# A recommendation tower on one core: the last chunk in two halves of 128 batches

## The reference

```
e = stack([tbl_f[ids[:, f]] for f in range(26)], axis=1)
sd = einsum('bfd,bd->bf', e, dense);  ss = einsum('bfd,bgd->bfg', e, e)
z = concat([dense, sd, ss[:, iu, ju]], axis=1);  h = concat([z, dense], axis=1)
h = max(h @ W_top1 + b_top1, 0);  h = max(h @ W_top2 + b_top2, 0);  y = h @ W_top3
```

## Time and profile before

| what | value |
|---|---|
| median of three runs | 566.14 us |
| profiled execution | 558.6 us, its span 556.8 us |
| TensorE, matmuls (PE) | 401.6 us busy, 72% of the span |
| TensorE, weight loads (PEld) | 361.3 us busy, 65% |
| ScalarE (ACT) | 211.6 us busy, 38% |
| VectorE (DVE) | 186.7 us busy, 34% |
| GpSimd (POOL) | 258.0 us busy, 46%, nearly all gathers (264) |
| mean granted TensorE clock | 0.859 of full speed |

### The profile page before, as it was taken

The page is one execution under the profiler, slowest core; times in us unless marked ns, Lnnn a source line. Parts: engine busy times, 40 slices in busy tenths (PEclk is TensorE's granted clock), DMA queues, the critical chain, the costliest instruction groups (busy, mean ns, idle before and its releaser), DMA issues.

```text
span 556.8 us, 9727 instructions
## 1 busy us (share of the span) xinstructions
PE 401.6 (72%) x3976; PEld 361.3 (65%) x3976; DVE 186.7 (34%) x684; ACT 211.6 (38%) x312; POOL 258.0 (46%) x270
## 2 busy tenths in 40 slices
PE   2603957777449869787849895688749887597898
PEld 2602856677338858577737895487747876496776
DVE  3503934263201544034420462124520355132300
ACT  3402733344313343334333352335334344255422
POOL 6774866336752266614664256524665256300000
PEclk9955896888778898879888997789888898799699
DMA  7951133325210152102511053102521042102030
GB/s 184 249 136 52 44 82 102 109 55 150 60 38 25 36 143 69 46 13 64 149 47 39 21 132 88 40 25 47 146 69 38 21 107 86 29 3 66 25 87 2
DMA packets 44509, 40.70 MB, mean 73 GB/s; under 512 B 29943, under 2 KB 36335, under 8 KB 44464
## 3 DMA queue, kind: packets, MB, share of 16 engines
q1 hardware_dynamic: 36016, 22.75, 15.8%
q0 software_dynamic: 8448, 17.32, 12.0%
HBM read 34.29 MB, written 5.76 MB: 72 GB/s over the span
## 4 chain that ended last, share of the span: by engine, by line
PE 53%; another core or an unknown queue 15%; issue 14%; ACT 8%; DVE 6%; DMA 2%; SPq 1%; DVEq 0%; ACTq 0%
PE oh_ps L590 23%; PE dot_ps L609 14%; PE mlp_ps L634 7%; DVE onehot L518 5%; PE mlp_ps L645 4%; PE tr_ps L575 4%; ACT feat L418 3%; ACT feat L423 2%; PE mlp_ps L653 1%; ACT ids_bc L407 1%; DMA dots<-tbl_dram 1%; DVE table_lo L505 1%; DMA dots_scratch<-rows 1%; ACT h L438 1%
## 5 line engine op out<-in xcount | busy, mean ns | idle before, releaser
L382 POOL DMA_INDIRECT rows<-tbl_dram,idx_sb x264 | 257.5, 975 | 220.8 <-PE tr_ps L575 101.2
L518 DVE TENSOR_SCALAR onehot<-ids_bc 125x256 fp32r<-125x256 int16 x608 | 137.9, 298 | 159.6 <-issue 53.6
L590 PE MATMUL oh_ps<-onehot,table_hi 125*128 125x256 f32 x608 | 106.8, 324 | 63.6 <-issue 30.8
L590 PEld LDWEIGHTS oh_ps<-onehot,table_hi 125*128 125x128 f32 x608 | 90.8, 220 | 70.8 <-issue 37.5
L423 ACT ACTIVATE feat<-oh_ps 128x256 f32<-128x256 f32 x76 | 51.8, 690 | 157.9 <-remote 66.5
L590 PE MATMUL oh_ps<-onehot,table_lo 125*128 125x256 f32 x608 | 96.2, 305 | 2.3 <-issue 2.1
L609 PE MATMUL dot_ps<-feat 128*54 128x52 f32 x2048 | 77.1, 235 | 23.2 <-issue 21.4
L590 PEld LDWEIGHTS oh_ps<-onehot,table_lo 125*128 125x128 f32 x608 | 88.6, 214 | 3.5 <-issue 3.1
L609 PEld LDWEIGHTS dot_ps<-feat 128*54 128x54 f32 x2048 | 69.6, 150 | 31.8 <-issue 27.6
L418 ACT ACTIVATE feat<-tr_ps 128x512 f32<-128x512 f32 (+1 forms) x72 | 82.5, 1146 | 15.4 <-remote 9.3
L527 DVE COPY dots<-dot_ps 54x416 f32<-54x416 f32 x56 | 32.2, 593 | 161.4 <-remote 123.4
(11 more groups left out here) (26 smaller groups left out, 72.6 us busy)
## 6 DMA issues: line engine op xcount, KB each, us to landing
dots_scratch<-dots SPq DMA_DIRECT2D x28, 175.5 KB
rows<-tbl_dram,idx_sb POOLq DMA_INDIRECT x264
ids_bc<-ids_t_dram SPq DMA_DIRECT2D x12, 256.0 KB
feat<-tbl_dram SPq DMA_DIRECT2D x6, 480.0 KB
zt<-dots_scratch SPq DMA_DIRECT2D x14, 117.0 KB
dots<-tbl_dram SPq DMA_DIRECT2D x3, 480.0 KB
ids_bc<-ids_t_dram SPq DMA_DIRECT2D x4, 320.0 KB
dense_sb<-dense_f_dram SPq DMA_DIRECT2D x8, 128.0 KB
```

The source lines that it names most:

```text
L382: nc.gpsimd.indirect_dma_start(rows[:, g, t, :], None, tables[UNIT[par][u][k]], bass.IndirectOffsetOnAxis(ap=idx_sb[:, par, g * TILES + t: ...
L518: last = nc.vector.tensor_scalar(onehot[0:TP, lookup_place(u), c, :], ids_bc[0:TP, u, :], float(c), None, ALU.is_equal)
L590: last = nc.tensor.matmul(lookup_psum(u), part[0:TP, u, c * D:(c + 1) * D], onehot[0:TP, lookup_place(u), c, :], start=(part is table_hi a ...
```

## The change

The last chunk is cut into two halves of 128 batches. Its gathers are issued for all units' first halves (t = 0) and then for the second (t = 1); a second half waits for nothing else on GpSimd. New step letters stand for its parts: a0 to a8 and b0 to b8 transpose and copy the first and the second half of each unit; e0 to e7 are its dot products, of which e0 to e3 make the first half and e4 to e7 the second; p0 to p5 are chunk 6's MLP; q and t are the MLP of the first and of the second half, with products that move 128 batches. `SLOT_LAST` now holds all of it and the three lists behind it are gone. SyncE stores and loads each half by itself (`make_last_z`), with the same number of DMAs for each half as before for the whole chunk but the dense load, which is issued once, ahead. Chunk 7's dots are copied to `dots` instead of `rows`, after chunk 6's stores from there have landed. On the host, the dense features and the outputs of the last chunk are reordered to match.

```diff
-SLOT_LAST = "m0 m1 r0 m2 m3 r1 m4 d0 d1 m5 d2 d3 l5 r2 d4 d5 l6 d6 d7 l7 r3 l8 r4 f r5 r6 r7 r8"
-DOTS = "d0 d1 d2 d3 d4 d5 d6 d7"
-MLP = "m0 m1 m2 m3 m4 m5"
+SLOT_LAST = ("m0 m1 m2 m3 m4 d0 d1 m5 d2 d3 l5 a0 d4 d5 l6 a1 d6 d7 l7 a2 l8 f a3 a4 a5 a6 a7 a8 e0 e1 e2 e3 "
+             "p0 b0 p1 b1 b2 p2 b3 p3 b4 b5 p4 b6 b7 p5 b8 e4 e5 e6 e7 q0 q1 q2 q3 q4 q5 t0 t1 t2 t3 t4 t5")
...
+        def columns(half):
+            return slice(0, CH) if half is None else slice(half * P, (half + 1) * P)
...
         def dots_of(h, par):
-            if isinstance(h, int) and chunk(h, par) == NCH - 1:
-                return rows[:].rearrange("p f t d -> p (f t d)")[:, 0:PACK * NJ * QS]
             return dots[:]
...
+            def make_last_z(half):
+                h, par = NCH // 2 - 1, 1
+                z, done = z_of(h, par), GUNITS * (NCH - 1) + GUNITS // 2 * (half + 1)
+                if half == 0:
+                    sp.wait_ge(dots_out_act, GUNITS * (NCH - 1))
+                    sp.dma_start(z[:, ZC, :], dense_t[NCH - 1:NCH].rearrange("a p b -> (a p) b")
+                                 ).then_inc(last_z_loaded[half], DMA)
+                sp.wait_ge(dots_out_act, done)
+                sp.wait_ge(dots_out_dve, done)
+                products = dots_dram[par, 0:NI * NJ, columns(half)].rearrange("(i j) b -> i j b", j=NJ)
+                w = QS // 2
+                for q in range(Q):
+                    row = TILE * (q // PACK) + NI * (q % PACK)
+                    own = dots[row:row + NI].rearrange("p (k j g) -> p k j g", k=PACK, j=NJ)
+                    sp.dma_start(products[:, :, q * w:(q + 1) * w],
+                                 own[:, q % PACK, :, half * w:(half + 1) * w]).then_inc(dots_stored, DMA)
+                sp.wait_ge(dots_stored, Q * DMA * (NCH + half))
+                for c in range(ZC):
+                    i0, m = c * ZI, min(ZI, NF - 1 - c * ZI)
+                    runs = dots_dram[par, i0 * (NJ + 1) + 1:(i0 + m) * (NJ + 1) + 1, columns(half)]
+                    sp.dma_start(z[0:m * DIST, c, columns(half)],
+                                 runs.rearrange("(i d) b -> i d b", d=NJ + 1)[:, 0:DIST, :]
+                                 ).then_inc(last_z_loaded[half], DMA)
...
+            def last_gathers(h, par):
+                pool.wait_ge(idx_loaded[par], DMA * (h + 1))
+                for t in range(TILES):
+                    for u in range(UNITS):
+                        if t == 0:
+                            pool.wait_ge(transposed, (chunk(h, par) - 1) * UNITS + u + 1)
+                        for k in range(len(UNIT[par][u])):
...
+            def last_transposed_to_feat(u, t):
+                act.wait_ge(transposed, (NCH - 1 + t) * UNITS + u + 1)
+                fs = UNIT[1][u]
+                m, step = len(fs), fs[-1] - fs[0]
+                nc.scalar.activation(feat_view(1, fs[0] + 1, m, max(step, 1))[:, :, t * P:(t + 1) * P],
+                                     tr_ps[:, 0:m, t * P:(t + 1) * P], ACT.Copy).then_inc(transposed_out, 1)
...
+            def last_transposes(u, t):
+                par, loads = 1, [DMA * TILES * len(UNIT[p][u]) for p in range(2)]
+                if t == 0:
+                    pe.wait_ge(rows_loaded[u], sum(loads) * (NCH // 2 - 1) + loads[0] + loads[par] // TILES)
+                else:
+                    pe.wait_ge(late_rows_loaded[u], loads[par] // TILES)
+                pe.wait_ge(transposed_out, (NCH - 1 + t) * UNITS + u)
...
             def dot_products(h, par, v):
                 n = chunk(h, par)
+                if n == NCH - 1 and v == GUNITS // 2:
+                    pe.wait_ge(transposed_out, UNITS * (NCH + 1))
...
-            def layer1(h, par, x):
...
+            def layer1(h, par, half, x):
+                n, cols = turn(h, par, half), columns(half)
                 if x == 0:
-                    if n < NCH - 1:
+                    if half is None:
                         pe.wait_ge(z_loaded, DMA * Z_DMAS * (n + 1))
                     else:
-                        pe.wait_ge(last_z_loaded, DMA * Z_DMAS)
+                        pe.wait_ge(last_z_loaded[half], DMA * (Z_DMAS - half))
```

More of the change, by code:

```diff
@@ L162, in z_of, with turn, h2_half @@
             return zt[:]
-        def h2_half(h, par, x):
-            return z_of(h, par)[:, x, :]
+        def columns(half):
+            return slice(0, CH) if half is None else slice(half * P, (half + 1) * P)
+        def turn(h, par, half):
+            return chunk(h, par) + (half or 0)
+        def h2_half(h, par, x, half):
+            return z_of(h, par)[:, x, columns(half)]
         def lookup_place(u):
@@ L182, in dlrm_tower @@
         rows_loaded = [sem(f"rows_loaded{u}") for u in range(UNITS)]
+        late_rows_loaded = [sem(f"late_rows_loaded{u}") for u in range(UNITS)]
         dense_loaded = sem("dense_loaded")
@@ L204, in dlrm_tower @@
         z_loaded = sem("z_loaded")
-        last_z_loaded = sem("last_z_loaded")
+        last_z_loaded = [sem(f"last_z_loaded{x}") for x in range(2)]
         l1_done = sem("l1_done")
@@ L444, in relu2, with output @@
                                      bias=b2_sb[:, x:x + 1]).then_inc(h2_made, 1)
[L446 to L449, removed]
+            def output(h, par, half):
+                n, cols = chunk(h, par), columns(half)
+                t0, t1 = cols.start // P, cols.stop // P
+                act.wait_ge(l3_done, turn(h, par, half) + 1)
+                nc.scalar.activation(y_sb[:, n * TILES + t0:n * TILES + t1], mlp_ps[:, 0, t0:t1],
@@ L481, in run @@
                         mlp_step(*old, x)
+                    if kind in "ab":
+                        last_transposed_to_feat(x, "ab".index(kind))
+                    if kind == "p":
+                        mlp_step(*done, x)
+                    if kind == "e":
+                        dots_to_sbuf(*rows, x)
+                    if kind in "qt":
+                        mlp_step(*rows, x, "qt".index(kind))
             act.wait_ge(iotas_made, 1)
@@ L524, in dots_to_sbuf @@
                 dve.wait_ge(dots_done, n * GUNITS + v + 1)
-                if v == 0 and not (isinstance(n, int) and n in (0, NCH - 1)):
+                if v == 0 and n:
                     dve.wait_ge(dots_stored, Q * DMA * n)
@@ L576, in transposes @@
                 last.then_inc(transposed, 1)
+            def last_transposes(u, t):
[5 more added lines that the diff above has]
+                pe.wait_ge(transposed_out, (NCH - 1 + t) * UNITS + u)
+                for k in range(len(UNIT[par][u])):
+                    last = nc.tensor.transpose(tr_ps[:, k, t * P:(t + 1) * P], rows[:, 2 * u + k, t, :], ident[:])
+                last.then_inc(transposed, 1)
             def lookup(h, par, u):
@@ L627, in layer1 @@
                         pe.wait_ge(y_made, n)
-                if x == 1 and not first:
+                if x == 1 and n:
                     pe.wait_ge(h2_made, n * (N2 // P))
@@ L633, in layer1, with layer2 @@
                     m = ZR if c < ZC else P
-                    last = nc.tensor.matmul(mlp_ps[:, x % 2, 0:CH], w1_sb[0:m, c, x * P:(x + 1) * P],
-                                            z_of(h, par)[0:m, c, :], start=(c == 0), stop=(c == ZC))
+                    last = nc.tensor.matmul(mlp_ps[:, x % 2, cols], w1_sb[0:m, c, x * P:(x + 1) * P],
+                                            z_of(h, par)[0:m, c, cols], start=(c == 0), stop=(c == ZC))
                 last.then_inc(l1_done, 1)
-            def layer2(h, par):
-                n = chunk(h, par)
+            def layer2(h, par, half):
+                n, cols = turn(h, par, half), columns(half)
                 for x in range(N2 // P):
@@ L712, with halved @@
             idx[n, :, 2 * u:2 * u + len(fs)] = unit_ids.transpose(1, 2, 0)
+    def halved(a):
+        return a.reshape(Q, 2, QS // 2, -1).transpose(1, 0, 2, 3).reshape(CH, -1)
+    dense_z = np.stack([dense[n * CH:(n + 1) * CH] for n in range(NCH - 1)] + [halved(dense[-CH:])])
     place = {ab: row for row, ab in enumerate((a, b) for a in range(NF) for b in range(a + 1, NF))}
```

98 lines of the change are left out of this document (57 added, 41 removed).

## The result

The changed kernel takes 572.36 us (median of 21 runs), the kernel before 566.14 us (21 runs). The ratio is 1.0176, 95% interval 1.0137 to 1.0214: 10 us slower (7.8 to 12.1). It is taken from the runs of each kernel within 1.5% of its fastest one, 16 of 21 after and 6 of 21 before, while the medians of all 21 lie only 6.2 us apart. The profiled execution of after is a long one (span 580.4 us). Its unchanged chunks already run behind: the stores of chunk 4 begin at 402.3 us against 385.6. So the two spans aren't to be subtracted, and what follows compares stretches of the end.

The account below looks back on a forecast made before the run. TensorE was taken to bound the kernel until about 509 us, then end stages without slack. The end's +12.6 us, e0's 2.4 us earlier start and -2.5 for gathers gave +7.7: 573.8 us, range 567 to 582.

Parts of the forecast that it names:

- e0 earlier by 2.4 us: Transposes before the last chunk's first dots: shorter half steps start e0 2.4 us earlier, 0.5 to at best 3.5.
- e0 to e4, 24.0 us: First half's dots, 5.8 us, then chunk 6's MLP interleaved with b0 to b8, 18.2 us: e4 starts 24.0 us after e0.
- e4 to e7, 4.8 us: Second half's four dot steps and a copy: 4.2 us at 2.4 GHz, 5.4 at a lowered clock, 4.8 taken.
- The way of half 1, 11.2 us: Second half's way through DRAM: 11.2 us, between 10.0 and 12.4, against 12.4 before for the whole chunk.
- q 7.3, t 9.2 us: MLPs of the two halves: 7.3 us for the first; 9.2 for the second, 1.9 of it from low clock after idling.
- The end as a whole, +12.6 us: From e0 to the output: 49.2 us against 36.6, since chunk 6's MLP no longer hides the way through DRAM.
- Gathers, -2.5 us: Reordered gathers in the slots before the end: between -9.7 and +7 us, -2.5 taken as half the balance of -4.9.
- Rival B: Run of 20 gathers holds up dots d0 to d3: gathers cost +4 to +7 us, total +14 to +17; chance 0.28.
- Rival A: Fewer early gathers bring -9.7 us instead of -2.5 and pay for the change: not slower, about 563 us; chance 0.14.

Follow-up runs that it names:

- the order with everything covered: Changed kernel's halves with all half transposes spread before the last lookup, gathers by unit, then e0 to e7, p, q, t; 0.9954 of the kernel before.
- gathers by unit: Changed kernel with the last chunk's gathers in the order of before, both halves of a unit behind that unit's wait; 1.0253 of the kernel before.

## Why the prediction was right

I forecast +7.7 us and 573.8 us; measured are 572.36 us, +10 by the ratio and +6.2 by the medians of all runs. Point by point:

- *e0 earlier by 2.4 us.* Of these 1.6 were meant for the stage of transposes (-1.9 and +0.3). From the last lookup to e0 are 8.1 to 8.6 us instead of 9.7: 1.1 to 1.6 us. The half steps are 1.26 us apart at first, but 1.51 once the clock has fallen (0.50 in 530 to 532 us), more than the 1.25 to 1.4 that I took. The other 0.8, transposes gone from the busy stretch, lies in the slots below.
- *e0 to e4, 24.0 us.* Measured 23.0. The waits before b2, b5 and b7 are there (1.00 us each, not 1.15), as are the slow first dots: 5.4 us, where I carried over 5.8, which by the earlier trace rows should have been 5.9.
- *e4 to e7, 4.8 us.* 4.24: the granted clock was 1.00 through them and through the stretch with b6 to b8 ahead; in the run with p behind e7, where TensorE was busy for 10.08 of 14.90 us ahead of them, it was 0.61.
- *The way of half 1, 11.2 us.* 10.06, the lower end of my range. Three store issues before the last take 2.4 us instead of 3.4, the landing 3.23 instead of 4.23, and 3.23 or 3.24 in four more traces. The packets of the stores are 128 B instead of 256, and as many. So halving the bytes did shorten this way, by 2.3 us in all. The Trainium skill ("DMA: Bandwidth & Descriptors", Specifications) says that transfers under 512 B are read, modified and written. That the stores would gain nothing by halving was my inference, which the page doesn't state, and these rows contradict it.
- *q 7.3, t 9.2 us.* 6.95 and 9.15. 32 passes of layer 1 take 3.84 us, 0.12 each, against 0.226 for 256 columns. The 81 ns for 128 columns in the Trainium skill ("TensorE: Matmul & The Clock Gate", Back-to-back issue gap) aren't reached by this float32 work.
- *The end as a whole, +12.6 us.* +9.9: the four terms were each a little too long, by 1.0, 0.6, 1.1 and 0.05. The mechanism, that chunk 6's MLP no longer covers the last way through DRAM, is shown by the run in which t doesn't wait (-6.3 us from e0 to the output) and by the order with everything covered (35.3 us).
- *Gathers, -2.5 us.* The two slots together: -1.9 in the profiled runs, -5.7 and +3.8. Taking off the 0.8 for the moved transposes, about -1.1 are left for the gathers, and the comparison with gathers by unit has 1.5. I had -9.7 and up to +7 and took half of a balance, which was a guess. Neither part was right: a gather that is taken away gives back 1.1 us, not 0.69, and a shift of them gives back much less than their sum. Rival B's late d0 is there, by 15 us, but the slot is only 3.8 us longer. It would last 42.7 us without its late gathers, so in the kernel before, too, some 15 of its 58.0 us came with gathers, in other places. Rival A's relief is there with -5.7 of its -9.7. That the balance came out near -2.5 is luck.

The rows give 9.9 - 1.1 - 1.9 = +6.9 us, against my 7.7. That the two are so near is partly luck as well: the end was forecast 2.7 us too long, and the rest 1.9 us too favourable. The medians of all runs agree with the rows (+6.2), the ratio is above them (7.8 to 12.1), by one to five us that no row accounts for. They are small beside what the unchanged first chunks do: the stores of chunk 4 begin between 382 and 402 us in the traces from the slower chips.

## What to carry to other kernels

Before cutting the last piece in halves, look at what runs beside its way through memory today. Here that was the MLP of the piece before, and moving this ahead of the last dots laid the way bare; the same halves in an order that keeps the cover cost nothing like it. But the halves themselves brought nothing: the one order with them that was not slower than before (0.9954) had its transposes spread as well, and whole chunks with spread transposes had 0.9894. The slack of this end was in a stage paced by ScalarE with TensorE idle, and it was to be had by reordering one list, with no new instruction: 0.9894 and 0.9907 of the time before.

## What the runs showed of the hardware

- In two traces of the changed kernel TensorE's dot products are recorded mostly 0.7 to 2.1 us apart while GpSimd issues a run of 20 gathers, and layer 2 ahead of them is picked up up to 10 us late; with the gathers in another order it is layer 1, by some 11 us. So MLP steps aren't spared, as my forecast and one expectation had it. Taking 17 gathers away gave back 1.1 us each. On a chip on which the kernel before takes 393 instead of 557 to 566 us nothing of it shows (the eight dot steps of chunks 1 to 6 take 11.6 us, where the kernel before has 15.6 to 17.1 for chunks 1 to 5). There the last slot takes 44.7 us with all its gathers and spread transposes, near the 42.7 of the other kind of chip without the 17, which fits the gathers as the larger part of the difference between the chips. A chip's own behaviour can thus be worth some seventeen times what the change does. What causes it wasn't found.
- Float32 passes of 128 columns take 0.12 us, of 256 columns 0.226; halving the batches halves layer 1 almost fully (3.84 against 7.19 us).
- The way through DRAM shrinks by a fifth when the bytes are halved and the packets stay as many: 10.06 us against 12.38.
- After 3.94 us without work the granted clock was 0.50 (1.2 GHz), and t's first layer took 6.04 us instead of q's 3.84; in four more traces with this wait it took 5.88 to 6.25. The low clock was worth 2.0 to 2.4 us each time.
